# Cross attention 3 on one Trainium2 core: maxima two heads at a time in two bank pairs, exponentials over two banks and one by turns in three banks

## The reference

```
x = x + L3_xattn(layernorm(x), ctx_1024, ctx_1024, mask, Wq, bq, Wk, bk, Wv, bv, Wo, bo)

q, k, v = heads(Q @ Wq.T + bq), heads(K @ Wk.T + bk), heads(V @ Wv.T + bv)   # 16 heads of 8
scores  = einsum('bhqd,bhkd->bhqk', q, k) / sqrt(8)
scores  = where(mask == 0, -1e9, scores)
attn    = softmax(scores, axis=-1)          # 1024 queries x 6404 keys, for each head
ctx     = einsum('bhqk,bhkd->bhqd', attn, v)
return ctx @ Wo.T + bo
```

## Time and profile before

| what | value |
|---|---|
| median of three runs | 6965.2 us |
| the profiled execution, its own time | 6964.83 us |
| its span in the profile | 6963.1 us |
| PE, DVE, ACT, POOL busy, of the span | 85%, 47%, 46%, 27% |
| maxima, scores and exponentials of cross attention 3 | from 5532 to 6700 us of the span |
| granted TensorE clock over the whole span | 0.904 |

### The profile page before, as it was taken

One profiled execution on the slowest core, in us unless ns is written; L12 is line 12 of the kernel. 1 busy time (PEld: TensorE's weight loads), 2 busy tenths in 40 slices (PEclk: granted clock), 3 DMA queues, 4 the chain that ended last, 5 costly groups with the idle time before them and its releaser, 6 DMA issues. The chain is left out here.

```text
span 6963.1 us, 76588 instructions
## 1 busy us (share of the span) xinstructions
PE 5944.1 (85%) x30204; PEld 2276.6 (33%) x30219; DVE 3275.8 (47%) x4563; ACT 3212.5 (46%) x3531; POOL 1903.2 (27%) x845
## 2 busy tenths in 40 slices
PE   8975999999999999979869569998888368888879
PEld 5741333333333333336624121111356111111114
DVE  4557555555555553034363430000232799899813
ACT  3321444444444445422202249998111137777752
POOL 0000878788787889900000000000000000000000
PEclk8875999999999999989989789999776679999979
DMA  1000000000000000000021030000000300000000
GB/s 47 4 13 0 1 1 1 1 1 1 1 1 1 1 1 1 1 28 7 9 92 34 17 101 16 16 9 7 16 30 8 118 1 9 18 9 9 2 17 31
DMA packets 91699, 118.19 MB, mean 17 GB/s; under 512 B 23358, under 2 KB 66729, under 8 KB 89741
## 3 DMA queue, kind: packets, MB, share of 16 engines
q1 hardware_dynamic: 91340, 113.29, 5.2%
HBM read 75.86 MB, written 37.39 MB: 16 GB/s over the span
## 5 line engine op out<-in xcount | busy, mean ns | idle before, releaser
L2417 DVE TENSOR_REDUCE red<-ps 128x2 f32<-128x1024 f32 (+1 forms) x832 | 976.9, 1182 | 965.7 <-PE ps L2235 963.8
L2354 ACT ACTIVATE Pr<-ps,key_bias 128x1024 f32<-128x1024 f32 x816 | 897.5, 1115 | 1112.9 <-PE ps L2250 1112.5
L2474 POOL TENSOR_TENSOR Ps<-Ps,Pr 128x1024 f32<-128x1024 f32 x400 | 944.1, 2360 | 318.0 <-ACT Pr L2354 318.0
L2910 DVE TENSOR_REDUCE red<-ps 128x2 f32<-128x1024 f32 (+2 forms) x1102 | 961.4, 926 | 79.3 <-PE ps L2825 66.2
L2483 POOL TENSOR_TENSOR Ps<-Ps,Pr 128x1024 f32<-128x1024 f32 x400 | 948.4, 2371 | 32.7 <-ACT Pr L2354 32.7
L492 POOL MEMSET sel<- 16x2048 f32 (+1 forms) x2 | 2.7, 1368 | 3402.9 <-POOLq L89 3402.9
L2888 ACT ACTIVATE Pr<-ps 128x1024 f32<-128x1024 f32 x816 | 786.2, 1021 | 224.6 <-PE ps L2835 223.6
L2248 PE MATMUL ps<-Q,Kr 64*128 64x512 f32 x3264 | 851.8, 600 | 0.0
L2267 PE MATMUL ps<-Pr,Vc 128*64 128x512 f32 x3264 | 789.8, 605 | 0.0
L3011 ACT ACTIVATE Pr<-ps 128x1536 f32<-128x1536 f32 x544 | 732.7, 1495 | 2.7 <-PE ps L2977 2.3
L2825 PE MATMUL ps<-Kp,Q 52*128 52x512 bf16 (+1 forms) x1664 | 449.8, 410 | 226.8 <-DVE red L2910 149.3
(11 more groups left out here) (487 smaller groups left out, 6596.9 us busy)
## 6 DMA issues: line engine op xcount, KB each, us to landing
L_dram_K<-parts SPq DMA_DIRECT2D x26, 384.0 KB, 2.8
Kp<-L_dram_K SPq DMA_DIRECT2D x16, 624.0 KB
L_dram_K<-parts SPq DMA_DIRECT2D x26, 256.0 KB, 2.3
Kp<-L_dram_K SPq DMA_DIRECT2D x16, 416.0 KB
w<-L_ffn_experts_w_dram SPq DMA_DIRECT2D x24, 256.0 KB, 3.0
L_dram_V<-Vt SPq DMA_DIRECT2D x13, 258.0 KB, 2.8
Vc<-L_dram_V SPq DMA_DIRECT2D x13, 258.0 KB, 2.7
ctx<-ctx_dram SPq DMA_DIRECT2D x13, 256.0 KB, 5.8
```

The source lines that it names most:

```text
L2354: nc.scalar.activation(Pr[:, t % 4, half].rearrange("p a n -> p (a n)"), ps[:, 2 * half:2 * half + 2, :].rearrange("p a n -> p (a n)"), AC ...
L2417: nc.vector.tensor_reduce(red[:, g % 2, q, :], ps[:, maxima_bank(g, q):maxima_bank(g, q) + 2, 0:ctx.keys_in(g % C)], AX, ALU.max).then_inc ...
L2474: nc.gpsimd.tensor_tensor(into, into, src, ALU.add).then_inc(*summed0.up())
L2910: nc.vector.tensor_reduce(red_flat[:, g % 2, first:first + n], ps[:, b:b + n, 0:ctx.keys_in(g % C)], AX, ALU.max).then_inc(*reduced.up())
```

## The change

After the change the scores have banks 0, 1 and 2, the maxima banks 3, 4 and 5, 6 as two pairs, and the products bank 7. Maxima are always units of two heads, eight in a chunk. The score matmuls are numbered through, item i = 4t + 2·half + a, and item i goes to bank i % 3. They are grouped into steps v: an even v takes two items (banks 0 and 1), an odd v one (bank 2), and each step has one exponential over 1024 or 512 columns. Step v waits for the exponential of step v - 2. Pr is a ring of 18 slots of 512 columns in place of 4 x 4.

```diff
-    N, LAG = P * C, C + 1
+    N, LAG, T = P * C, C + 1, P * KT
+    first = lambda v: 3 * (v // 2) + 2 * (v % 2)
+    step_of = lambda i: 2 * (i // 3) + (i % 3 == 2)
...
-    Pr = k.tile(stack, "Pr", [128, 4, 2, 2, HALF])
+    Pr = k.tile(stack, "Pr", [128, 18, HALF])
...
-        n = len(units(g)) if g < N else 0
+        n = 8 if g < N else 0
...
-        def maxima(i, u):
-            first, n, b = units(i)[u]
-            p = i // C
-            take_banks(b, reduced.at(unit_number(i, u) + 1))
+        def maxima(i, q):
+            p, b = i // C, 3 + 2 * (q % 2)
+            take_banks(b, reduced.at(8 * i + q + 1))
...
-        def scores(j, s, half):
...
-            take_banks(2 * half, exp_done.at(2 * t + half + 1))
-            for a in range(2):
-                mm = nc.tensor.matmul(ps[:, 2 * half + a, :], lhsT=Kp[head(a), p % 3, kt * 128:(kt + 1) * 128], rhs=Q[head(a), p, HALVES[half]], start=True, stop=True)
+        def scores(v):
+            if v >= 2:
+                nc.tensor.wait_ge(*exp_done.at(v - 1))
+            for i in range(first(v), first(v + 1)):
+                t, half, a = i // 4, i // 2 % 2, i % 2
+                p, kt = t // KT, t % KT
+                if kt == 0 and i % 4 == 0:
+                    nc.tensor.wait_ge(*rows_set.at(2 * p + 2))
+                mm = nc.tensor.matmul(ps[:, i % 3, :], lhsT=Kp[head(a), p % 3, kt * 128:(kt + 1) * 128], rhs=Q[head(a), p, HALVES[half]], start=True, stop=True)
             mm.then_inc(*scored.up())
...
                 if p:
                     nc.tensor.wait_ge(*out_copied.at(p))
...
+            nc.tensor.wait_ge(*exp_done.at(step_of(4 * t + 3) + 1))
             for half in range(2):
-                nc.tensor.wait_ge(*exp_done.at(2 * t + half + 1))
...
             nc.tensor.wait_ge(*rows_step.at(3 * p + 3))
-            take_banks(4, rows_set.at(2 * p + 2))
+            take_banks(3, rows_set.at(2 * p + 2))
+            take_banks(5, rows_set.at(2 * p + 2))
...
+                ready = [v for v in range(made, made + 4) if 0 <= j < N and first(v + 1) - 1 <= 4 * t + 3]
+                made += len(ready)
                 items = maxima_at(g, s, steps)
...
+                for q in items[:1]:
+                    maxima(g, q)
+                for v in ready[:2]:
+                    scores(v)
+                for q in items[1:]:
+                    maxima(g, q)
+                for v in ready[2:]:
+                    scores(v)
+                while step_of(4 * done + 3) <= made - 3:
+                    products(done)
+                    done += 1
...
     def act():
...
+                while 0 <= j < N and first(made + 1) - 1 <= 4 * t + 3:
+                    i, n = first(made), first(made + 1) - first(made)
+                    nc.scalar.wait_ge(*scored.at(made + 1))
+                    if i + n - 1 >= 18:
+                        nc.scalar.wait_ge(*weighed.at((i + n - 1 - 18) // 4 + 1))
+                    nc.scalar.activation(Pr[:, i % 18:i % 18 + n, :].rearrange("p a n -> p (a n)"), ps[:, i % 3:i % 3 + n, :].rearrange("p a n -> p (a n)"),
+                                         ACT.Exp).then_inc(*exp_done.up())
+                    made += 1
...
-                if s == 0 and j > 0 and j % C == 0:
+                if j > 0 and j % C == 0 and s == (1 if j < N else 0):
                     p = j // C - 1
                     nc.scalar.wait_ge(*weighed.at(KT * (p + 1)))
...
-                    nc.scalar.copy(Oc[:, p % 2, :], ps[:, 6, :]).then_inc(*out_copied.up())
+                    nc.scalar.copy(Oc[:, p % 2, :], ps[:, 7, :]).then_inc(*out_copied.up())
```

More of the change, by code:

```diff
@@ L2806, in pe @@
     def pe():
[L2807 removed]
+        taken = {3: None, 5: None}
         def take_banks(b, when_free):
@@ L2822, in maxima @@
             at = (i % C) * CHUNK
-            for item in range(first, first + n):
-                q, a = item // 2, item % 2
-                mm = nc.tensor.matmul(ps[:, b + item - first, 0:keys], lhsT=Q[head(a), p, q * 128:(q + 1) * 128], rhs=Kp[head(a), p % 3, at:at + keys], start=True, stop=True)
+            for a in range(2):
+                mm = nc.tensor.matmul(ps[:, b + a, 0:keys], lhsT=Q[head(a), p, q * 128:(q + 1) * 128], rhs=Kp[head(a), p % 3, at:at + keys], start=True, stop=True)
             mm.then_inc(*maxima_mm.up())
-        def scores(j, s, half):
[L2829 to L2832, removed]
-            take_banks(2 * half, exp_done.at(2 * t + half + 1))
-            for a in range(2):
-                mm = nc.tensor.matmul(ps[:, 2 * half + a, :], lhsT=Kp[head(a), p % 3, kt * 128:(kt + 1) * 128], rhs=Q[head(a), p, HALVES[half]], start=True, stop=True)
+        def scores(v):
[7 more added lines that the diff above has]
+                mm = nc.tensor.matmul(ps[:, i % 3, :], lhsT=Kp[head(a), p % 3, kt * 128:(kt + 1) * 128], rhs=Q[head(a), p, HALVES[half]], start=True, stop=True)
             mm.then_inc(*scored.up())
@@ L2859, in pe @@
         nc.tensor.wait_ge(*zeroed.at(1))
+        made = done = 0
         for g, j, steps in turns():
@@ L2862, in pe @@
                 t = KT * (j // C) + TPC * (j % C) + s
+                ready = [v for v in range(made, made + 4) if 0 <= j < N and first(v + 1) - 1 <= 4 * t + 3]
+                made += len(ready)
                 items = maxima_at(g, s, steps)
[L2864 to L2875, removed]
+                for q in items[:1]:
[9 more added lines that the diff above has]
+                    done += 1
                 if s == 1 and g % C == 0 and 0 < g <= N:
                     rows(g // C - 1)
+        for t in range(done, T):
+            products(t)
     def act():
+        made = 0
         for g, j, steps in turns():
@@ L2907, in dve @@
                 nc.vector.wait_ge(*merged.at(g - 1))
[L2908 to L2911 removed]
+            for q in range(8):
+                b = 3 + 2 * (q % 2)
+                nc.vector.wait_ge(*maxima_mm.at(8 * g + q + 1))
+                nc.vector.tensor_reduce(red[:, g % 2, q, :], ps[:, b:b + 2, 0:ctx.keys_in(g % C)], AX, ALU.max).then_inc(*reduced.up())
+            nc.vector.wait_ge(*reduced.at(8 * g + 8))
             if g % C == 0:
```

25 lines of the change are left out of this document (4 added, 21 removed).

## The result

| | before | after |
|---|---|---|
| median | 6963.2 us (4 runs) | 7014.0 us (4 runs, 7010.3 to 7031.3) |
| ratio to before, 95% interval | | 1.0075, 1.006 to 1.0089 |
| first merge of the maxima to the last copy of the products | 1157.7 us | 1213.1 us |

The kernel is 0.75% slower; 7008 was predicted. The profiled execution after took 7031.3 us. 11 of its 67 us more lie outside the stage, and executions differ there by tens of us (the first merge stands at 5519 to 5558 us in this case's profiles). The stage's own length, last row, repeats to 0.4 us between two executions of the kernel after. It grew by 55.4 us, and it is the better measure for the experiments.

A forecast was written before the change was run, and what follows sets the result against it. It took VectorE, 91% busy in the middle part, to set the pace before the change. Forecast: 6964.8 + 21 (middle part, passes included) + 22.5 (last part) = 7008 us, with 8 in 10 for 6945 to 7055.

The forecast's parts named there:

- The turn: Middle part: three tiles of TensorE's written order take 7.65 us, 2.55 a tile against 2.54 before; 118 turns, 903 us.
- Both holds: Twice a turn TensorE waits for a refill until its own tile's exponential is over, 0.67 and 0.46 us.
- The reason given for it: In the turn, products of 0.98 us stand right behind the refill wait, so the 75 us gain is given back entirely.
- The pass between pairs: Where one pair of heads follows another: 9.0 us more for each of six passes, 54 us in all.
- The copy's wait: At a pass, the zero matmul waits 1.7 us for the products' bank copy behind the new pair's fifth exponential.
- a rival: TensorE's clock halves behind the copy wait, +3 us on seven passes (7029), or throughout the last part (7073); chance 0.18.
- The last part: Final stretch without maxima: 2.27 us a tile against 1.86, +20.5 on 50 tiles, and one copy +2: +22.5 us.
- The first part: Opening stretch of maxima alone, two bank pairs in place of three: no cost, 0 to +1.5 us at its end.
- VectorE's need: In the middle part's turn of 7.65 us, VectorE needs 6 x 1.13 = 6.78 us and stands still for the rest.
- VectorE at full pace: First rival: VectorE keeps the middle part's pace, refills coming sooner or hiding behind maxima; -75 us there, 6907; chance 0.10.
- The signs: If right: merges 10.1 to 10.3 us apart, VectorE idle some 10%, TensorE holds 0.5 to 0.7 us, last-part turns 6.8.
- sign of being wrong: Merges 9.3 to 9.6 us apart, or a last part under 112 us, or clocks of 0.5 in it.

The follow-up runs named there:

- e3: Kernel after, with every reduction from the 15th chunk on over the first 256 keys of each head only; stage 1193.8 us, 1.0059 of kernel before.
- e6: Kernel after, with every exponential over the first 256 columns of each bank only; chunk 9.26 us, stage 1108.9 us, 0.993 of kernel before.
- e2: Kernel after, with products of the tile two before put ahead of the last scores step in every tile; stage 1184.7 us, 1.0034 of kernel before.
- e5: Kernel after, products one tile later, ahead of the last scores step only in the second of three tiles; stage 1177.7 us, 1.0018 of kernel before.
- e1: Kernel after, with the products' bank copy put back behind the exponentials of the new pair's first tile; stage 1183.2 us, 1.0051 of kernel before.
- e4: Kernel after, with the old 11 maxima units of two heads and one from the 15th chunk on; stage 1318.9 us, 1.0233 of kernel before.
- e9: Kernel after, one-bank exponentials in seven pairs, products between third and fourth item, copy earlier, last pair six banks, three per exponential; 0.9958 of kernel before.
- e7: Kernel after, unchanged, run again beside the others; stage 1213.5 us, 1.0072 of kernel before.
- e8: e4 with its reductions from the 15th chunk on over the first 256 keys only; stage 1236.4 us, 1.0109 of kernel before.

## Why the prediction was right

Its steps, against the runs:

- **The turn.** Predicted 7.65 us, measured 7.56. Both holds are there, in the second and third tile, 0.61 and 0.62 us where 0.67 and 0.46 stood. e3 shows that VectorE is not the pace and e6 that the exponential's length is. This term decided the case, and it was the one worked out from the order and the prices. 118 turns came to some 892 us, not 903.
- **The reason given for it** was half right. "The products of 0.98 stand right behind that wait" is true of the rows, but e2 shows that moving them frees nothing. What binds, by the prices that the walk used, is a chain of four wide links a turn: from a wide step's scores to the next scores in the same banks at least 0.43 + 1.12 = 1.55 us, and of the four gaps between wide steps three at most can be filled by products. That is worked out and fits e2, e5 and e6; no run took the fourth gap away by itself.
- **The pass between pairs.** The copy's wait was predicted at 1.7 us and is 1.60 by the row; its clock was left to a rival, at +3 us a pass. That part of the rival came true in every pass: the rows beside e1's give 2.5. The middle part is therefore 962.5 long, not 955: 11 us less by the turns, some 18 more by the passes, 15 of these the clock of six.
- **The last part.** Predicted 2.27 us a tile and +22.5; 2.23 and +25. The turns, 50 tiles at 0.37 more, are only 18.5 of it. The copy's wait and the half clock behind the last copy (6648.24 to 6658.8) are 2.4, the difference to e1's last part. Some 4 us more were priced nowhere, and no run divides them.
- **The first part** +1, predicted 0 to 1.5.
- **VectorE's need** of 6.78 us a turn left out the merges; by the earlier trace rows it is 6.95. Nothing hung on it, since both are under the turn.
- **The rivals.** VectorE at full pace would have needed a turn of 6.95; e6 shows what that takes. The last part did not fall to half clock as a whole: the window that holds it stands at 0.96.
- **The signs.** Most came: a zero matmul that waits, holds of 0.6 us in each second and third tile, turns of 6.69 us in the last part (6.8 expected) with ScalarE at 86% (84). Chunks are 9.82, 10.14 and 10.26 by turns, mean 10.07, just under the 10.1 to 10.3 named, and VectorE idles 14% of the middle part, not 10. One sign of being wrong came too: a clock of 0.5 in the last part, for the 10 us behind its copy.

On the clock the prediction cites the Trainium skill, "TensorE: Matmul & The Clock Gate", "A second HAM failure mode: psum-queue depth-cycling", which says that short idles between groups of matmuls that cycle through PSUM banks can make it swing. In the steady turn, with two such holds of 0.6 us, this trace does not agree; the clock falls at the passes, where TensorE has stood 1.6 to 2.1 us for a copy or a cast (behind such a wait it does not always fall, as the last section tells):

```profile
5700.00:5780.00 80.00, 71.56 (x508) 16.22 (x508) 75.26 (x72) 64.43 (x86) 0.00 (x0) 1.00 0.00 1
```

```profile
5800.00:5815.00 15.00, 9.91 (x66) 1.97 (x58) 9.55 (x9) 8.75 (x12) 0.00 (x0) 0.77 0.12 46
```

Above is the kernel after in steady turns, below at a pass.

So the mechanism of the forecast was right, and that its sum, 7008, came within 6 us of the median was in part luck. The turns were priced 11 us too long, the passes and the last part together some 20 too short, and the stage grew by 55.4 us where 43.5 was forecast; the rest is the spread outside the stage.

## What to carry to other kernels

When buffers move from one stream to another, price the chain that each buffer closes: fill, wait, use, release, fill. Compare it with the work that the in-order engine has between the two fills. If it is longer, the engine stands, and everything behind stands with it, whoever was the bottleneck before. Holds by two different partners in one queue can add up, as e4 shows. And if the chain is too long for the buffers, look first at its longest member (narrower operations, refilled further apart) and then at the order of the queue: here order alone brought 0.13 us a chunk (e5), narrow operations with an order to suit them 0.59 (e9).

## What the runs showed of the hardware

An exponential of 512 f32 columns takes 596 ns; four of them run in 2.06 us, 0.49 from one to the next, where one of 1024 columns follows the last after 0.93 and one of 1536 after 1.35 ((90.41 - 1.49) / 66). So 512 columns more cost about 0.43 us, and the fixed part between successors is only some 0.06 us; of a single one it is 0.17 (0.596 - 0.43). That is why 1428 narrow exponentials cost ScalarE little.

After the copy's wait of 1.60 us the zero matmul ran at 0.60, half clock, at all seven copies of the kernel after and at all seven of e7. Behind the same wait six of seven in e3 ran at full clock, five of seven in e4 and four of seven in e8; behind a wait of 1.17 us in e6 all seven did. One of e3's:

```profile
6207.22 0.38 PE L2830 MATMUL ps<-zero_row 1*128 1x512 bf16 x1 [1.60 <-ACT Oc L2895]
```

There the clock fell a little later: the next maxima, at 6208.91, take 0.61 us each, and the matmuls stay at half for 6 us. So the length of the last wait alone does not decide it. What does was not tried.
